# The mixture of a two-layer decoder in split float32r products, its expert weights split ahead during the first layer's feed-forward

## The reference

```python
gate = x @ W_gate + _lora(x, sA_gate, sB_gate, scale) + _expert_lora(x, A_gate, B_gate, w, scale)
up = x @ W_up + _lora(x, sA_up, sB_up, scale) + _expert_lora(x, A_up, B_up, w, scale)
hidden = jax.nn.silu(gate) * up
```

```python
expert_idx = jnp.argmax(logits, axis=-1)
score = jax.nn.sigmoid(jnp.max(logits, axis=-1))
xs = x * score[:, None]
for e in range(n_experts):
    m = (expert_idx == e)[:, None]
    xe = jnp.where(m, xs, 0.0)
    h = jax.nn.silu(xe @ gate_w[e]) * (xe @ up_w[e])
    out = out + jnp.where(m, h @ down_w[e], 0.0)
shared = jax.nn.silu(x @ shared_gate_w) * (x @ shared_up_w) @ shared_down_w
```

## Time and profile before

| what | us |
|---|---|
| median of 3 runs (3343.5 to 3350.7) | 3348.0 |
| profiled execution, its own time | 3358.8 |
| its span, first to last instruction | 3356.9 |
| TensorE busy (matmuls) | 2993.0, 89% |
| VectorE, ScalarE, GpSimd busy | 1613.5, 1276.2, 617.4 |
| mean granted TensorE clock | 0.952 |
| first feed-forward, about | 1065 to 1665 |
| mixture, first row load to end | 2879 to 3357 |

### The profile page before, as it was taken

How to read it: one execution, slowest core, us unless ns; L and a number is a source line. 1 busy time by engine, 2 the same in 40 slices (tenths; PEclk the granted TensorE clock), 3 DMA queues, 4 the chain that set the end, 5 groups by cost and what they waited for, 6 DMA issues and landing times. The chain is left out here.

```text
span 3356.9 us, 47726 instructions
## 1 busy us (share of the span) xinstructions
PE 2993.0 (89%) x16242; PEld 2018.0 (60%) x16274; DVE 1613.5 (48%) x3127; ACT 1276.2 (38%) x3279; POOL 617.4 (18%) x699
## 2 busy tenths in 40 slices
PE   7999858888884999999979986899999999899998
PEld 6677623233332777777745553788888888644443
DVE  5655657667661211111136664566667666211222
ACT  3443416555562111111125553555565555211111
POOL 0000031232221000000010011333333333200332
PEclk9999969999885999999989998999999999899999
DMA  2000076756743200000010021101221110522342
GB/s 76 13 25 25 7 170 131 150 131 130 163 96 124 64 14 13 14 13 14 7 47 26 25 69 57 38 26 50 69 70 52 50 50 26 192 64 88 111 172 75
DMA packets 129471, 229.71 MB, mean 68 GB/s; under 512 B 17061, under 2 KB 34789, under 8 KB 129296
## 3 DMA queue, kind: packets, MB, share of 16 engines
q1 hardware_dynamic: 104688, 180.37, 19.7%
q0 software_dynamic: 13936, 31.98, 3.2%
q10 hardware_dynamic: 10672, 15.04, 1.4%
HBM read 167.68 MB, written 61.00 MB: 68 GB/s over the span
## 5 line engine op out<-in xcount | busy, mean ns | idle before, releaser
L1418 DVE TENSOR_REDUCE x_minus_max<-banks 128x2 f32<-128x1024 f32 x256 | 308.1, 1223 | 165.8 <-PE banks L1484 164.0
L1366 ACT ACTIVATE x_probs<-banks 128x512 f32<-128x512 f32 x512 | 272.5, 597 | 159.8 <-PE banks L1502 145.4
L580 ACT ACTIVATE a_probs<-banks,a_minus_max 128x128 f32<-128x128 f32 (+1 forms) x512 | 208.3, 430 | 96.9 <-DVE a_minus_max L676 96.2
L1502 PEld LDWEIGHTS banks<-x_stacked_q,x_stacked_k 53*128 53x128 f32 x512 | 64.9, 202 | 214.4 <-issue 162.8
L1502 PE MATMUL banks<-x_stacked_q,x_stacked_k 53*128 53x512 f32 x512 | 162.3, 532 | 31.3 <-ACT x_probs L1366 23.2
L2248 POOL TENSOR_TENSOR x_probs<-x_probs,x_inverse 128x512 f32<-128x512 f32 x128 | 133.1, 1040 | 266.7 <-DVE x_inverse L2454 266.7
L2312 ACT ACTIVATE x_probs<-banks,x_minus_max,x_rroot 128x256 f32<-128x256 f32 x256 | 142.9, 566 | 87.5 <-DVE x_minus_max L2420 87.5
L1484 PE MATMUL banks<-x_stacked_k,x_stacked_q 51*128 51x512 f32 x512 | 137.6, 485 | 39.9 <-DVE x_whole L1435 13.2
L676 DVE TENSOR_REDUCE a_minus_max<-banks 128x2 f32<-128x512 f32 (+1 forms) x192 | 131.7, 686 | 84.0 <-remote 65.5
L3083 PE MATMUL banks<-m_w,m_xT 128*128 x368 | 167.3, 598 | 4.0 <-issue 4.0
L1835 DVE TENSOR_TENSOR f_hT<-banks,f_silu 128x256 f32<-128x256 f32 (+1 forms) x88 | 37.2, 424 | 267.4 <-ACT f_silu L1748 267.4
(11 more groups left out here) (384 smaller groups left out, 7762.6 us busy)
## 6 DMA issues: line engine op xcount, KB each, us to landing
x_parts_dram<-x_parts SPq DMA_DIRECT2D x16, 1024.0 KB, 6.0
x_x<-x_after SPq DMA_DIRECT2D x24, 512.0 KB, 4.1
x_stacked_k<-x_parts_dram SPq DMA_DIRECT2D x96, 128.0 KB
x_stacked_q<-x_parts_dram SPq DMA_DIRECT2D x96, 128.0 KB
x_after<-a_z SPq DMA_DIRECT2D x16, 512.0 KB, 2.7
x_z<-x_after SPq DMA_DIRECT2D x16, 512.0 KB, 6.5
x_heads_dram<-x_heads_out SPq DMA_DIRECT2D x32, 256.0 KB
x_after<-x_z SPq DMA_DIRECT2D x16, 512.0 KB, 3.4
```

The costliest lines, as they stand in the source:

```text
L580: ins = act.activation(probs[:, n % 3, i * width:(i + 1) * width], psum[uses.bank(use)][:, i * width:(i + 1) * width], ACT.Exp, bias=minus ...
L1366: act.activation(probs[:, n % 8, :], psum[at.bank(f"exp{n}")], ACT.Exp, scale=SCALE)\
L1418: dve.tensor_reduce(minus_max[:, c % 2, h % 4:h % 4 + 2, t], at.pair(use), AX.X, ALU.max, negate=True)\
L1502: ins = pe.matmul(psum[at.bank(use)], stacked[1][u][rows, h // 2, s * P:(s + 1) * P].bitcast(F32R), stacked[0][u][rows, h // 2, :].bitcast ...
```

## The change

1. **The mixture's products are split.** Each of the four f32 matmuls of a product becomes three float32r ones. ScalarE rounds x and hT (`x_high`, `hT_high`), VectorE subtracts (`rest_of_x`, `rest_of_h`). Shared tiles still read the transposed x from `xT_all`, but through the two parts. VectorE's `normalise` moves out of `give_y`, behind `rest_of_h`.
2. **Weights arrive as high part and rest**, 2 MB a matrix, from a scratch tensor `expert_parts` in HBM. The three buffers double (the tile `w` now lies over the space of `xT_all`, so that expert 1's up part waits until all shared x are split). Gate, up and down parts have a semaphore each per buffer; SP asks for each when the product that used it is done for the last time, and each product waits for its own part.
3. **The weights are split in the first feed-forward.** 27 matrices (8 experts and the shared one, three each) and one dummy are 28 pieces of 1 MB. Four pieces in each sequence but the first are handled at the blocks j = 1, 4, 7, 10: ScalarE rounds into `expert_high`, VectorE subtracts in place in `expert_rest`, GpSimd stores both, waits for both, and loads the next piece but one. The host lays the matrices out in rows of 8 KB per partition.

```diff
+        expert_rest = [raw_up_first[:, :, :].rearrange("p c n -> p (c n)")[:, k * KC * D:(k + 1) * KC * D] for k in range(2)]
+        expert_high = sb("expert_high", [P, KC * D])
+        EXPERT_PIECES_AT = ({1: 0, 4: 1, 7: 2, 10: 3}, {1: 4, 4: 5, 7: 6, 10: 7})
...
+            def load_expert_piece(piece, slot):
+                pool.dma_start(expert_rest[slot], expert_raw[piece].rearrange("a p n -> (a p) n"))\
+                    .then_inc(expert_loaded[slot], 16)
+            def store_expert_piece(turn, c):
+                g = expert_piece(turn, c)
+                pool.wait_ge(expert_split, g + 1)
...
+                pool.dma_start(expert_parts[bass.ds(g, 1), 0].rearrange("a p n -> (a p) n"), expert_high[:, :])\
+                    .then_inc(expert_high_stored, 16)
+                pool.dma_start(expert_parts[bass.ds(g, 1), 1].rearrange("a p n -> (a p) n"), expert_rest[c % 2])\
+                    .then_inc(expert_rest_stored, 16)
+            def follow_expert_piece(turn, c):
+                g = expert_piece(turn, c)
+                pool.wait_ge(expert_high_stored, g * 16 + 16)
+                pool.wait_ge(expert_rest_stored, g * 16 + 16)
+                pool.sem_inc(expert_high_free, 1)
+                load_expert_piece(bass.ds(g + 2, 1), c % 2)
...
+            def sequence(turn, u):
+                for c in EXPERT_PIECES_AT[u].values():
+                    store_expert_piece(turn, c)
+                    follow_expert_piece(turn, c)
+                norm_pool(core, norm, turn, u)
...
+                act.wait_ge(expert_loaded[c % 2], turn * (8 * PER_TURN) + 16 * ((c - SKIPPED) // 2 + 1))
+                act.wait_ge(expert_high_free, g + 1)
+                high_part_act(act, expert_high[:, :], expert_rest[c % 2]).then_inc(expert_rounded, 1)
...
+                dve.wait_ge(expert_rounded, expert_piece(turn, c) + 1)
+                subtract(dve, expert_rest[c % 2], expert_rest[c % 2], expert_high[:, :]).then_inc(expert_split, 1)
...
-        w = sb("w", [P, BUFFERS, 3, KC, D])
+        w = sb("w", [P, BUFFERS, 3, 2, KC, D])
...
+                for m, used in enumerate((gate_full, up_full, y_full)):
+                    if e == BORROWED and m == 1:
+                        sp.wait_ge(x_split, NT)
+                    if e == SHARED:
+                        sp.wait_ge(used, NT)
+                    if e >= BUFFERS:
+                        sp.wait_ge(used, done[e - BUFFERS])
+                    load_weight(e, m, expert_loaded[m][e % BUFFERS])
...
+            def rest_of_h(t):
+
+                u = t % 2
+                dve.wait_ge(hT_rounded, t + 1)
+                if t >= 2:
+                    dve.wait_ge(y_full, t - 1)
+                subtract(dve, hT_rest[:, u], psum[XT + u].rearrange("p (c t) -> p c t", c=KC), hT_high[:, u]).then_inc(hT_ready, 1)
...
                 if t >= 1:
                     give_y(t - 1)
+                rest_of_h(t)
+                if t >= 1:
+                    normalise(t - 1)
...
-                    ins = pe.matmul(psum[bank], parts[:, c, :], weight(buffer, m, c), start=c == 0, stop=c == KC - 1)
+                    ins = split_matmul(pe, psum[bank], [part[:, c, :] for part in parts],
+                                       [weight(buffer, m, part, c) for part in range(2)], start=c == 0, stop=c == KC - 1)
```

More of the change, by code:

```diff
@@ L2660 @@
 BUFFERS = 3
+EXPERT_PIECES = 28
 FACTS = 1 + BUFFERS
-COPIES = 48
+COPIES = 16
 META = 4
@@ L2687, in mixture_pads, with mixture_weights, mixture @@
     return pads
-def mixture(core, name, x_src, x_dst, base, slot_meta, weights):
+def mixture_weights(inputs):
+    import numpy as np
+    pieces = np.zeros((EXPERT_PIECES + 2, P, KC * D), np.float32)
+    for m, key in enumerate(("gate_w", "up_w", "down_w")):
+        for e in range(E + 1):
+            w = inputs["L1_ffn_" + key][e] if e < E else inputs["L1_ffn_shared_" + key]
+            pieces[e * 3 + m] = np.asarray(w).reshape(KC, P, D).transpose(1, 0, 2).reshape(P, KC * D)
+    return pieces
+def mixture(core, name, x_src, x_dst, base, slot_meta, parts_src, weights):
     nc, psum = core.nc, core.psum
@@ L2754, in mixture @@
         shared_loaded = ring_of("shared_loaded", 3)
-        expert_loaded = ring_of("expert_loaded", BUFFERS)
+        expert_loaded = [ring_of(f"expert_{part}_loaded", BUFFERS) for part in ("gate", "up", "down")]
         filled = sem("filled")
@@ L3094, in down @@
                     pe.wait_ge(y_ready, t - 1)
-                product(DOWN + u, hT[:, u], buffer, 2, y_full)
+                wait_expert(2, needs)
+                product(DOWN + u, (hT_high[:, u], hT_rest[:, u]), buffer, 2, y_full)
             chosen_flat = chosen_bf[:, :, :].rearrange("p t e -> p (t e)")
@@ L3107, in facts_of, with wait_expert @@
                 return fact(0, s), [fact(1 + k, s) for k in range(BUFFERS)]
[L3109 removed]
+            def wait_expert(m, needs):
+                for k, need in enumerate(needs):
+                    pe.wait_ge(expert_loaded[m][k], need)
+            previous, before_needs, buffer, needs = None, [], None, []
             for t in range(LAST + 1):
                 u, s = t % 2, t - NT
[L3112 to L3116 removed]
+                source = x_high[:, u], x_rest[:, u]
+                pe.wait_ge(x_split, t + 1)
+                wait_expert(0, needs)
                 if t == 0:
@@ L3138, in _ @@
                 if t >= 1:
-                    down(t - 1, previous)
+                    down(t - 1, previous, before_needs)
                 if t >= 1:
                     transpose_h(t)
-                previous, (buffer, needs) = buffer, following
-            down(LAST, previous)
+                previous, before_needs, (buffer, needs) = buffer, needs, following
+            down(LAST, previous, before_needs)
 def decoder_layers(nc, a, x, result):
@@ L3166, in decoder_layers @@
         feed_forward_lora(core, "f0", between[1], between[2],
-                          group("f0", "first", "gate", "up", "down", "B_gate", "B_up", "A_down", "B_down", "bias"))
+                          group("f0", "first", "gate", "up", "down", "B_gate", "B_up", "A_down", "B_down", "bias"),
+                          a["m1_all"], expert_parts)
         with ExitStack() as both:
@@ L3174, in decoder_layers @@
             cross_attention_grouped(core, "x1", between[3], a["ctxT"], between[4], half_way, x1_weights, early)
-        mixture(core, "m1", between[4], result, base, slot_meta, group("m1", "r", "g", "u", "d", "sg", "su", "sd", "table", "pads"))
+        mixture(core, "m1", between[4], result, base, slot_meta, expert_parts, group("m1", "r", "table", "pads"))
 def layout(inputs):
```

140 lines of the change are left out of this document (97 added, 43 removed).

## The result

The changed kernel took 3310.8 us (median of 4 runs, 3299.6 to 3317.8) beside 3349.4 for the kernel before: ratio 0.987, interval 0.9848 to 0.9892. Faster, as forecast, but by 43 us by the ratio and not by 64.5, and outside the range (3264 to 3304). Two later comparisons of the same two kernels gave 0.9833 and 0.9853. The profiled execution went from 3358.8 to 3309.1 us, 49.8 less.

A forecast was written before the change was run, and what follows sets the result against it. TensorE's own work was taken to bound the mixture. Terms -74.3 - 6.2 + 14 + 1 + 1 = -64.5 us, taken off 3348, gave 3284 us, range 3264 to 3304.

The forecast's parts named there:

- the products: Mixture: each of 117 products takes 2.80 us as float32r where 3.435 were, -74.3 us.
- rival 3: Mixture's expert products: register writes hold up one-pass matmuls, products stay at 3.43 us; 3328 us, chance 0.05.
- the waits for weights: Mixture: TensorE's waits for an expert's weights and the stretched products after them all go, -6.2 us.
- TensorE's sequencer: Expert tiles: loading four facts delays the down product, 0.67 us in each of 21 tiles, +14 us.
- Rival 2: Expert tiles: the facts stay hidden, the sequencer sending faster or VectorE being released earlier; 3270 us, chance 0.22.
- the pieces cost TensorE nothing in their stage: First feed-forward: splitting weights in 28 pieces at a period of 11.9 us, in time below 12.7, booked 0.
- The forecast's own sign: First feed-forward: TensorE's idle time ahead of the a_down products, 8.1 us in all, stays.
- the period did not come to 17: First feed-forward: stores landing one after the other, period 17 us, 3356 us, slower than before; chance 0.05.
- At the change to expert tiles ... +1 us: Mixture, from shared to expert tiles: VectorE's wait for gathered base rows meets a shorter tile and smaller burst, +1 us.
- the burst 1 MB (2.6 us) smaller: Change to expert tiles: the weights ahead of the gather of base rows shrink by 1 MB, 2.6 us.
- the first tile: Start of the mixture: h of tile 0 takes one pass more before the down product, +1 us.

The follow-up runs named there:

- again: The changed kernel run once more with no edit: 3299.9 us, ratio 0.9833 to the kernel before.
- facts_early: Changed kernel with the four facts of the next tile loaded ahead of the transposes of x, not behind the up product: 3291.2 us.
- rest_first: Changed kernel with VectorE, in expert tiles, subtracting hT's high part between y's sum and its statistics: 3284.6 us (median of five runs; 3288.2 with a sixth).
- down2_late: Changed kernel with SyncE asking for expert 2's down part only when the first four gathers of base rows have landed: 3301.1 us.
- sp_pieces: Changed kernel with the feed-forward pieces' loads and stores issued by SyncE and not by GpSimd: 3295.1 us, ratio 0.9838 to the kernel before.
- again_2: The changed kernel run a third time with no edit: 3304.5 us, ratio 0.9853 to the kernel before.
- stores_serial: Changed kernel with GpSimd asking for a piece's rest store only when its high part's store has landed: 3345.9 us, ratio 0.997 to the kernel before.

## Why the prediction was wrong, point by point

**Right: the products.** 2.79 us each where 2.80 was worked out, expert and shared; register writes (rival 3) cost nothing. Shared tiles come at 8.83 us (8.84 forecast). **Right: the waits for weights.** Both are gone (-6.2 us).

**Right, in mechanism and size: TensorE's sequencer.** Expert tiles came 9.92 us apart in again, 0.66 over the 9.26 without the wait, 20 times (the tile of the change counted with them): 13 us, where +14 was booked. TensorE's sequencer at one such place, between the up product sent and the down product:

```profile
L3213 PEldq TENSOR_LOAD <-m_slot_facts x4: 297/301/313, 3114.8 to 3116.7; - x4
L3213 PEldq SEQ_ASSERT  x4: 18/18/18, 3115.4 to 3117.3; - x4
```

2.5 us of facts, from 3114.8 to 3117.3, after the previous down product ended at 3110.7 and ahead of the next at 3117.7: 7.0 us where 7.1 was pieced together. Rival 2 (the facts stay hidden) is out, and facts_early and rest_first show both of its ends.

**Right: the pieces cost TensorE nothing in their stage**, at a period of 11.6 to 12.4 us but for single ones up to 13.8 (11.9 forecast; 12.7 was the bound worked out). The forecast's own sign holds: TensorE's idle time ahead of the product with A_down is 8.0 us in all, 8.1 before. ScalarE's roundings of one sequence in again:

```profile
1402.27 1.89 ACT L93 CAST f_expert_high<-f_raw_up_first 128x2048 fp32r<-128x2048 f32 x1
...
1413.99 1.91 ACT L93 CAST f_expert_high<-f_raw_up_first 128x2048 fp32r<-128x2048 f32 x1 [3.29 <-POOLq L1747]
...
1426.34 1.91 ACT L93 CAST f_expert_high<-f_raw_up_first 128x2048 fp32r<-128x2048 f32 x1 [4.54 <-POOLq L1747]
```

The changed kernel's issues (KB each, median us to landing) say why the period did not come to 17:

```profile
f_raw_up_first<-in_m_all POOLq DMA_DIRECT2D x30, 1024.0 KB, 5.1
expert_parts<-f_expert_high POOLq DMA_DIRECT2D x28, 1024.0 KB, 4.2
expert_parts<-f_raw_up_first POOLq DMA_DIRECT2D x28, 1024.0 KB, 6.1
```

The two stores overlap: the second, sent 0.6 us behind the first, lands after 6.1, the first after 4.2. So the pair takes 6.7 us. The Trainium skill ("DMA: Bandwidth & Descriptors", section "Bandwidth") gives 6.15 us for 1 MB moved from HBM to SBUF by GpSimd's DMA; the prediction asked what two stores would cost at that price, one behind the other. The trace does not agree with that use of it: a load of that size took 5.1 us, and a pair of stores 6.7 and not 12.3. The measurement decides.

**Wrong: "At the change to expert tiles ... +1 us".** It was 5.2 us in the first trace, 6.4 in again and 5 to 7 in the others, but for those with the edits of rest_first (4.4) and down2_late (0). The step that failed is "the burst 1 MB (2.6 us) smaller". The kernel before asks here for expert 2's 3 MB (three loads, the first at 3088.09) around its last store of base rows, and the gathers wait for that store:

```profile
3088.09 0.37 SPq L2827 DMA_DIRECT2D m_w<-in_m_g  x1
3088.82 0.33 ACTq L2930 DMA_DIRECT2D base_rows<-m_rows  x1
3096.61 0.94 POOL L2869 DMA_INDIRECT m_rows<-base_rows,m_source_row  x1 [121.04 <-DMA base_rows<-m_rows]
```

The changed kernel asks for 10 MB, five loads of 2 MB: expert 1's up and down parts, which now wait for the last shared x, and expert 2's three parts, which follow gate, up and down product of the last shared tile:

```profile
3044.26 22.73 SPq L2903 DMA_DIRECT2D m_w<-expert_parts  x5
```

It is the last of the five, 0.7 us ahead of the store, that holds it up (down2_late). From the store's issue to VectorE's sum are 11.9 us before (3088.82 to 3100.76), 13.1 in the changed kernel and 13.2 in again, where the forecast had 2.6 less than before. So VectorE's sum is 4.6 us late in again and not 0.8, which makes 3.8 of the 4.0 us that TensorE idles. The other 3.0 us are a second failed step, a term put at nothing: behind this idle time the transposes and two products run at a granted clock of 0.50. Together 7.0 us; 0.6 of them hide the wait for facts of this tile, which leaves 6.4.

**Wrong: the end of the feed-forward's block, booked at nothing.** GpSimd's DRAIN, +3.7 us, in a stage where I had looked only at TensorE's products (sp_pieces).

**Wrong: the end of the mixture, booked at nothing.** The last down product waits for VectorE's statistics and its rest of hT: TensorE idles 2.2 us and not 0.8. In six of the eight traces with these 2.2 us the product is then slow (4.31 to 4.62 us for 3.06; the granted clock is 0.67 over it in the first trace and 1.00 in again). 1.4 to 3.0 us; rest_first takes 0.7 back, and in none of the three traces with its edit (1.5 us idle) is the product slow.

**The sum with these terms.** The loop was to be 437.5 - 64.5 = 373.0 us. With 5.4 more for the change to expert tiles (6.4 and not 1), 1.4 for the end, 1 less for the facts and 0.2 less at the first tile it is 378.6; 378.5 was measured in again and 378.9 in again_2. With 3.7 for the block's end the change is worth 55 us.

**Wrong: from the sum to the predicted time.** The profiled execution of the kernel before lay 11 us over the median shown, and I took the sum off that median. The runs of the kernel before that were made for the experiments have medians of 3354 to 3360 us, so the profiled one was typical, and the runs behind the first median were low by 5 to 10 us. The changed kernel's four runs in that comparison were high: 3310.8 us, 3299.9 and 3304.5 in the later two. So the first comparison shows 38 us between medians, the other two 60 and 50. The one of its four runs that has a trace had the stall of 7 us at the third tile; whether the others had such stalls is open. The mean of the three ratios, 0.9852, is 50 us, 5 less than the sum. The slow last product in most traces is some 1 us of that; the rest is not explained, and each ratio's interval reaches 7 us to each side.

So the time fell outside the range by two causes that I had not put in it: 9 us in terms outside the places where I looked or priced too low, shown by the experiments, and some 17 us by which the first comparison falls short of that sum, runs that were low for one kernel and high for the other, whose cause is open. Around the typical base, 9 us higher, the same range (3273 to 3313) would have held the time with the same terms wrong: that would have been luck, and no proof of the terms.

## What to carry to other kernels

Price a wait of TensorE above its idle time once it reaches 2 us, in this case at 1.7 to 2.4 times the idle time: 4.1 us of idle time cost 2.7 more in the third tile, 4.0 cost 3.0 at the expert change, 2.2 cost up to 1.5 at the end (in six of eight traces), and 16 cost 23 in stores_serial; behind 1.5 us nothing was lost. When loads get bigger, list what is asked for just around every small transfer that somebody waits for, by time of issue, not by total bytes: 2 MB asked for 0.7 us ahead of a store cost 5.8 us, and the 8 MB asked for earlier 1 us at most (3.0 us where 2.0 is usual). And look at the ends of the blocks: an engine that gets DMAs to issue may leave its block later although its last DMA has long landed.

## What the runs showed of the hardware that I had not expected

GpSimd's DRAIN at the end of the feed-forward's block took 8.06 us in nine of nine traces where GpSimd had issued DMAs in the block's loop (in the changed kernel it began 11.7 us after the last of them was issued), and 1.24 us in four of four where it had issued only the loads at the block's start. Signals of TensorE reached ScalarE 8.3 us after the recorded end of its transposes, and VectorE 6.1 us after the end of a product, once in eleven traces of kernels with the change, at no known cause. Loading one fact into a register of TensorE's sequencer takes 0.63 us with its register operations, and in the four loads from 3114.8 to 3117.3 the sequencer has no other entry. A store of 256 KB landed after 2.0 us on an idle DMA and after 7.1 to 10.2 while 2 MB loads were under way (2.8 to 3.0 where the last of them ended within 2 us of its issue).
